# Masked scores of a graph attention: eight ScalarE activations per batch in place of one VectorE operation

## What is computed

```python
h = x @ Wr
s = h @ a_src
d = h @ a_dst
e = jax.nn.leaky_relu(s[src] + d[dst], negative_slope=NEG_SLOPE)
e = jnp.where(mask, e, -jnp.inf)
m = jax.ops.segment_max(e, dst, num_segments=N)
w = jnp.where(mask, jnp.exp(e - m[dst]), 0.0)
denom = jax.ops.segment_sum(w, dst, num_segments=N)
alpha = w / denom[dst]
msg = alpha[:, None] * h[src]
return jax.ops.segment_sum(msg, dst, num_segments=N) + br
```

## Time and profile before

| | us |
|---|---|
| median of 3 runs | 4712.49 |
| lowest, highest | 4703.44, 4718.89 |
| the profiled execution | 4667.5 |
| its span, first to last instruction | 4665.8 |
| of it the attention's turns (first to last copy of counts, L863) | 269.0 to 2181.8 |

### The profile page before, as it was taken

How to read it: one execution, slowest core, us unless ns; L and a number is a source line. 1 busy time by engine, 2 the same in 40 slices (tenths; PEclk the granted TensorE clock), 3 DMA queues, 4 the chain that set the end, 5 groups by cost and what they waited for, 6 DMA issues and landing times. The chain is left out here.

```text
span 4665.8 us, 82665 instructions
## 1 busy us (share of the span) xinstructions
PE 3351.8 (72%) x18946; PEld 2344.4 (50%) x18947; DVE 2627.3 (56%) x9544; ACT 1442.6 (31%) x3181; POOL 2313.0 (50%) x1837
## 2 busy tenths in 40 slices
PE   1535655555665555556476785899999999999993
PEld 0224444444444444444133232677777777777771
DVE  6157777777777777777666444343343344334332
ACT  0124443344443444433100000333333333333330
POOL 0145554555555454541000000588788778778871
PEclk9855555555555555555787776898898889889886
DMA  1353333323333233485533230355445445445443
GB/s 49 95 116 84 84 80 90 86 79 80 98 83 84 79 93 85 80 79 127 116 74 88 67 79 12 41 54 52 47 51 53 48 48 53 49 47 53 50 43 72
DMA packets 652004, 331.97 MB, mean 71 GB/s; under 512 B 436912, under 2 KB 610275, under 8 KB 650980
## 3 DMA queue, kind: packets, MB, share of 16 engines
q0 software_dynamic: 148736, 86.57, 19.6%
q1 hardware_dynamic: 485510, 143.62, 14.5%
q10 hardware_dynamic: 17568, 99.95, 5.3%
HBM read 158.05 MB, written 196.59 MB: 76 GB/s over the span
## 5 line engine op out<-in xcount | busy, mean ns | idle before, releaser
L1853 POOL DMA_INDIRECT sums<-el_rows,el_idx x816 | 1292.3, 1584 | 857.3 <-DVE el_rows L2068 619.3
L827 POOL DMA_INDIRECT at_hs<-table,at_rec_s x976 | 1012.3, 1037 | 917.9 <-DVE at_hw L1130 602.1
L863 ACT CAST at_count_s<-near_ps 128x400 f16<-128x400 f32 x976 | 480.3, 492 | 1212.7 <-remote 600.8
L972 PE MATMUL near_ps<-at_pair_hot,at_src_low_hot 128*128 128x400 f16 x976 | 480.8, 493 | 450.6 <-ACT at_count_s L863 298.0
L2066 DVE CAST el_idx<-el_place 128x4 uint32<-128x4 f32 x204 | 40.1, 197 | 939.1 <-DMA sums<-el_rows,el_idx 426.6
L946 PEld LDWEIGHTS sums_ps<-at_hw,at_hit 128*128 128x128 f32 x1952 | 471.8, 334 | 29.8 <-issue 29.5
L946 PE MATMUL sums_ps<-at_hw,at_hit 128*128 128x66 f32 x1952 | 442.4, 409 | 8.3 <-DVE acc L1016 8.3
L1916 PE MATMUL el_h_ps<-w,el_h 128*128 128x128 f32 x1632 | 443.5, 358 | 0.0
L972 PEld LDWEIGHTS near_ps<-at_pair_hot,at_src_low_hot 128*128 128x128 f16 x976 | 127.5, 131 | 627.8 <-ACT at_count_s L863 419.2
L1902 PE MATMUL el_h_ps<-el_ea_t,w1b 64*128 64x128 f32 x1632 | 432.7, 348 | 0.2 <-issue 0.2
L963 PE MATMUL near_ps<-at_count_s,carry_by 128*128 x244 | 102.5, 523 | 412.4 <-issue 366.6
(11 more groups left out here) (342 smaller groups left out, 5557.5 us busy)
## 6 DMA issues: line engine op xcount, KB each, us to landing
slots<-at_count_s ACTq DMA_DIRECT2D x122, 800.0 KB
chunk<-slots SPq DMA_DIRECT2D x480, 100.0 KB
el_rec<-attr SPq DMA_DIRECT2D x816, 32.0 KB
attr<-in_edge_attr SPq DMA_DIRECT2D x19, 1248.0 KB
at_rec_s<-meta SPq DMA_DIRECT2D x992, 3.5 KB
at_hs<-table,at_rec_s POOLq DMA_INDIRECT x976
el_pair<-meta SPq DMA_DIRECT2D x816, 1.0 KB
sums<-el_rows,el_idx POOLq DMA_INDIRECT x816
```

The costliest lines, as they stand in the source:

```text
L827: pool.indirect_dma_start(hs[:, s, u, :], None, k.table, bass.IndirectOffsetOnAxis(rec[:, s, u, 0:1].bitcast(U32), 0)).then_inc(gathered[s ...
L863: a.copy(count[:, (n.o + d) % 2, i, :], near[:, (n.o + d) % 2, 0:AW]).then_inc(count_ready, 1)
L972: pe.matmul(near[:, s, 0:AW], low_hot[:, s, i, :], pair_hot[:, s, i, :], start=False, stop=True, skip_group_check=(i > 0)).then_inc(near_r ...
L1853: pool.indirect_dma_start(k.sums_flat[a], bass.IndirectOffsetOnAxis(idx[:, j, a:a + 1], 0), rows[:, j, a, :], None, compute_op=ALU.add).th ...
```

## The change

`far` is made by ACT, with eight activations of 128x128 per turn, one for each visit, four before copy 0 and four before copy 1. An activation computes scale * in + bias; here the input is the mask `miss`, the scale -2^100 and the bias the column of scores in `hs`. DVE's operation over all eight visits goes, with its waits for the gathered rows, for `miss` and for ACT's last `hit`. ACT gets the first two of these waits. DVE gets a wait for `far_ready` before it writes `key` (and behind it `miss`) of batch n+2.

```diff
+            def fars(n, d, h):
+
+                s, q = (n.o + d) % 2, (n.o + d) % RING
+                if h == 0:
+                    act.wait_ge(gathered[q], (n.round(d) + 1) * (16 * B))
+                    act.wait_ge(key_step, n(5, 5 * d + 5))
+                for u in range(4 * h, 4 * h + 4):
+                    m = a.activation(far[:, s, u, :], miss[:, s, u, :], ACT.Identity, bias=hs[:, q, u, D + 1:D + 2], scale=-BIG)
+                if h == 1:
+                    m.then_inc(far_ready, 1)
...
             def step(n):
                 if n.has(1):
+                    fars(n, 1, 0)
                     keep(n, 1, 0)
+                    fars(n, 1, 1)
                     keep(n, 1, 1)
...
-                if n.has(1):
-                    q = (n.o + 1) % RING
-                    dve.wait_ge(gathered[q], (n.round(1) + 1) * (16 * B))
-                    dve.wait_ge(key_step, n(5, 10))
-                    if n.after(1):
-                        dve.wait_ge(hit_ready, n(2))
-                    v.scalar_tensor_tensor(far[:, w], miss[:, w], -BIG, hs[:, q, :, D + 1:D + 2].to_broadcast([P, B, P]),
-                                           ALU.mult, ALU.add).then_inc(far_ready, 1)
...
                         dve.wait_ge(deg_ready, n(1, 1))
+                        dve.wait_ge(far_ready, n(1, 1))
                     v.tensor_tensor(key[:, m], rec[:, q, :, 1], k.key_base[:, bass.ds(n(B, 2 * B), B)],
                                     ALU.subtract).then_inc(key_step, 1)
```

## The result

The changed kernel is slower: median 4805.34 us (4782.89 to 4830.94) against 4711.84 (4703.44 to 4718.89), a ratio of 1.020 with a 95% interval of 1.015 to 1.026. The profiled execution took 4782.89 us, against 4667.5 before: +115 us.

A forecast was written before the change was run, and what follows sets the result against it. The prediction took the PE-ACT chain to set the turn, with DVE following with slack. DVE -10, ACT 0 and POOL +78 gave +68 us, counted as 67, for 4780 us; the 8-in-10 range was 4655 to 4850.

The forecast's parts named there:

- the loss of holding: Without `far` on DVE, POOL's gathers are no longer held and turns lengthen: 78 us slower, chance 0.43.
- DVE's time: Rival: the length of DVE's turn counts after all, so less DVE work is faster, 4661 us; chance 0.32.
- Nothing: Rival: DVE's slack grows, ACT's work is covered, only 10 us remain, 4702 us; chance 0.20.
- holding is only a companion of short turns: Lower end of the POOL loss: held gathers accompany short turns without causing them, so nothing is lost.
- ACT on the chain: Rival: activations before copies 0 and 1 delay the PE-ACT chain by 2.4 us a turn, 5005 us; chance 0.05.
- POOL's term: Gathers in the attention: 56 us of holding by `far` lost, at 1.39 us of turn per us, 78 us slower.
- upper end: POOL's gathers: with a new rhythm later holdings are lost too, 87 us of holding x 1.39 = 121 us slower.
- DVE's term: DVE loses 1.22 us a turn, mostly covered by its wait for `hit_t`: 10 us gained.
- ACT's term: Eight added activations before copies 0 and 1, covered by PE's L946 matmuls: cost nothing.
- The signs to look for: Profile checks: gather mean falling towards 980 ns, turns 16.4 us or more, more DVE idle, ACT up 2.1 to 2.4 us.
- the forecast's failure: Condition that would refute the forecast: turns without any holding come out as short as the held ones.

The follow-up runs named there:

- e1: The changed kernel, with DVE again doing its old two-input operation at the old place into a tensor nobody reads: 4677.27 us, 1.001 of the kernel before.
- e2: The changed kernel, with a DVE operation of about the same length but one SBUF input at the old place: 4778.32 us, 1.021 of the kernel before.
- e10: The kernel before, plus a one-input DVE operation of the same length at the start of DVE's turn: 4643.38 us, 1.000 of the kernel before.
- e7: The kernel before, plus a second, unread two-input scores operation at the start of DVE's turn: 4510.08 us, 0.958 of the kernel before.
- e9: The changed kernel, plus the unread two-input DVE operation at both the turn's start and the old place: 4467.09 us, 0.962 of the kernel before.
- e3: The kernel before, plus ACT's eight activations a turn as unread extra work at their new places: 4683.78 us, 1.003 of the kernel before.
- e11: The kernel before, with DVE's `far` moved from behind the maximum to the start of its turn, nothing added: 4500.06 us, 0.968 of the kernel before.
- e4: The kernel before, with one POOL gather a turn in place of eight (other rows stale): 4285.60 us, 0.915 of the kernel before.
- e6: The changed kernel, with one POOL gather a turn in place of eight (other rows stale): 4125.14 us, 0.877 of the kernel before.

## Why the prediction was right, point by point

**Sign and mechanism.** The forecast was slower through the loss of holding, 4780 us in a range of 4655 to 4850; it came to 4805. e1 and e2 show that the loss of holding is the cause; that what it costs is late semaphores is read from the traces. *DVE's time* (4661) falls with e2 and e10, and with e7 and e9, which are faster with more of it. *Nothing* (4702) and "holding is only a companion of short turns" fall with e1 and e2. *ACT on the chain* (5005) falls with e3.

**POOL's term was mis-sized.** It was 56 us of holding x 1.39 = 78 us, under an upper end of 121; the attention lost 142 us. Both factors were low. First, I counted only the gathers held by `far` and held that "the rest of the holding falls to other DVE operations, which stay". The operations stayed and the holding didn't: (1037 - 953) ns x 976 = 82 us of it are gone, 82 of the 91 that there were (93 ns x 976). By overlap in the timelines some 22 of the 91 us lie beside `low_hot` and 10 beside `miss`: in the kernel before, a late gather met one of these, operations with two SBUF inputs, as here (a turn in its timeline):

```profile
1402.74 1.22 DVE L1110 TENSOR_TENSOR at_miss<-at_key,iota_mid 128x1024 bf16<-128x1024 f32 x1
1403.39 1.39 POOL L827 DMA_INDIRECT at_hs<-table,at_rec_s  x1 [0.30 <-issue]
```

In the turn of the changed kernel shown above DVE stands before `picked` until 1166.27, and so reaches `miss` only at 1171.12, when the last gather has been over since 1168.83. The first loss brings the second. That was the case of my upper end ("if with a new rhythm the later holdings are lost too"), and it should have been the middle. Second, the price: 142 / 82 = 1.73 us per us held, not 1.39, which came from one pair of turns. The trace of the kernel before had the better number. I take each of its 107 turns with eight gathers (those from 3 us before one last `pair_hot` to 3 us before the next) and add up what the gathers last beyond 944 ns. The 30 turns with under 0.1 us held have a median of 17.4 us, the 58 with 0.7 or more one of 15.0, and a straight line through all falls by 1.7 us per us held. In the changed kernel 102 of 116 turns have under 0.1 us held, and their median is 17.5. Nor is it one price. From e2 to e1 it is (16.56 - 15.63) / (0.89 - 0.06) = 1.1, from e10 to e11, where DVE also does 1.2 us less, (15.58 - 14.65) / (1.15 - 0.86) = 3.2. So the place seems to matter; I read it that a gather held just as PE finishes the last count and the picks is worth most, but no run tests that by itself.

**DVE's term** of -10 us can't be told apart from nothing. The idle time before the maximum did not grow. The saved time was waited away at the sum over `picked`, 120.8 / 106 = 1.14 us a turn where it had been 34.1 / 113 = 0.30, and before DVE's three waits for its own results, 2.4 us a turn where it had been 0.8. The prediction named the first, in 35 turns (it was 61), and not the others.

**ACT's term**, taken at 0, comes to some 14 us by e3 (0 to 26). ACT's busy time rose by 925.88 / 105.3 - 732.25 / 113.6 = 2.35 us a turn, in the forecast 2.1 to 2.4.

The Trainium skill, ScalarE: Activation LUTs, section "What ACT_TABLE_LOAD costs", gives by estimate 280 + 0.833 x 128 = 387 ns for one such activation; the trace has a mean of 391 ns. Its 93 ns of overlap would leave an estimated 294 each in a row, and the row above has 270.6 us / 848 = 319.

**What came by luck.** The untouched rest of the program ran 28 us shorter in the profiled execution after, within what it differs by from trace to trace (2456 to 2500 us). Without that the profiled execution would have gone up by 142 and not by 115, and the forecast of +67 would have looked as small as its POOL term was. The medians differ by 93 us.

**The signs to look for.** The gather's mean was to fall towards 980 ns; it fell to 952. Turns of 16.4 us or more: 16.86. No gather long at the start of a DVE turn: none in the turn shown, though a few are left (the longest of the stretch is 1957 ns). The wait of the sum over `picked` grew. And turns without holding did not come out short (17.4 and 17.5 us above), which would have been the forecast's failure.

**Still open.** Why semaphores come late while gathers run in a row. The runs show that the pauses go with the gathers (e4, e6) and that holding POOL by DVE relieves them (e1, e7, e11); in the turn shown they end near the row's last gather, DVE's own 1.7 us behind it. Whether what is in the way is the issuing or the transfers behind it, no run here tells. Nor did I try other ways to slow POOL than through DVE.

## What to carry to other kernels

Before taking an operation off the busiest engine, look at what its neighbours wait for, and at what that operation *holds*: here 1.22 us less of DVE a turn made the turn 1.17 us longer. In a kernel like this one, where an engine stands idle before a result that is already there ("remote" or "issue", several us), look for a stream of GpSimd-issued DMAs beside it, and place a two-input DVE operation against it rather than away from it, ahead of a wait and not behind it (3.2% for a move of five lines). The cheapest gauge of such a delay is an engine's wait for its own last result: 2.4 us a turn in the changed kernel, 0.8 before, nothing in e4. Test such a theory with a pair of dummies of the same length that differ in the one property, as e1 and e2 do.

## What the runs showed of the hardware that I had not expected

Seven of the eight indirect DMAs of a turn on POOL, with time to spare on POOL itself, cost this kernel 3.2 us of each 15.7 us turn and 8.5% of the whole (e4), although ACT's copies beside them keep their length (492 ns with and 494 without): the price is in waits for semaphores, between engines and of DVE for itself. The Trainium skill, SBUF — State Buffer, section "Who interferes with whom", has it that "PE and ACT never wait on anyone". It speaks of SBUF ports, and the traces say nothing against that. As a rule for the time it would mislead: ACT waited 6.12 us for a count that, by its modelled end, was there.

The holding itself is selective. A 1.22 us operation of two SBUF inputs stretched a gather from 0.94 to as much as 2.03 us; one of 1.21 us with a single SBUF input left it at its 951 ns mean. The Trainium skill, SBUF — State Buffer, section on the two separate sides, says that of two such operations the one that starts first gets the shared ports and the other fully blocks. For a gather that comes second the trace agrees (1.94 us for 0.94); for DVE it does not: `far` began 0.04 us behind a gather and took its usual 1.22 us. Nor is the blocking a loss here: e7 holds POOL 1.40 us a turn, nearly twice as long as the kernel before, and is 4.2% faster.
